# Other gates and another order in the lead-in of a fused attention and ternary-projection kernel on eight cores

## What is computed

```python
xn = _layernorm(x)
q = xn @ w_q + b_q; k = xn @ w_k + b_k; v = xn @ w_v + b_v     # [2, 16384, 1024]
scores = einsum(q, k of positions s-3 .. s+3) / 8              # outside the row: -inf
out = (softmax(scores) applied to v) @ w_o + b_o
scale = maximum(mean(abs(weight)), 1e-5)
w_ternary = clip(round(weight / scale), -1, 1)
result = x + out + xn @ (w_ternary * scale).T
```

## Time and profile before

| | us |
|---|---|
| median of 3 runs (range) | 695.19 (694.86 to 695.31) |
| the profiled execution | 696.35 |
| its span, slowest core (5) | 694.8 |
| spans of the 8 cores | 688.6 to 694.8 |
| PE busy | 644.1 (93%) |
| DVE busy | 434.4 (63%) |
| ACT busy | 375.5 (54%) |

### The profile page before, as it was taken

How to read it: one execution, slowest core, us unless ns; L and a number is a source line. 1 busy time by engine, 2 the same in 40 slices (tenths; PEclk the granted TensorE clock), 3 DMA queues, 4 the chain that set the end, 5 groups by cost and what they waited for, 6 DMA issues and landing times.

```text
span 694.8 us, 11677 instructions; the slowest of 8 cores (688.6 to 694.8 us)
## 1 busy us (share of the span) xinstructions
PE 644.1 (93%) x3890; PEld 299.8 (43%) x3890; DVE 434.4 (63%) x534; ACT 375.5 (54%) x1418; POOL 88.6 (13%) x52
## 2 busy tenths in 40 slices
PE   1669983999999999999999999999899999999996
PEld 1234431444444444444444444444344444455542
DVE  6225398686666667666665666666666755466663
ACT  3333465475555565656555555556556555555572
POOL 1202000221111111111111010011011111111110
PEclk9969996899999999999999999999999999999999
DMA  7699973768554444557563654544353442334423
GB/s 167 158 158 323 166 124 84 213 166 230 137 135 104 120 132 123 110 130 144 131 139 88 152 137 137 137 109 126 86 127 94 109 76 81 92 102 126 123 62 92
DMA packets 129947, 91.19 MB, mean 131 GB/s; under 512 B 107872, under 2 KB 116192, under 8 KB 129888
## 3 DMA queue, kind: packets, MB, share of 16 engines
q1 hardware_dynamic: 121440, 82.05, 45.9%
q0 software_dynamic: 8448, 8.39, 8.8%
HBM read 55.82 MB, written 16.78 MB: 104 GB/s over the span
## 4 chain that ended last, share of the span: by engine, by line
PE 83%; DVE 6%; DMA 4%; ACT 3%; issue 3%; DVEq 0%; SPq 0%; POOL 0%; ACTq 0%; POOLq 0%
PE p_p L284 16%; PE p_f L452 15%; PE p_p L302 15%; PE p_f L468 15%; PE p_p L327 15%; PE p_a L415 3%; PE p_s L355 3%; ACT sm L385 2%; DMA wq_b<-wq 1%; DVE sm L370 1%; DMA x<-x 1%; DMA sm<-x 1%; DVE bst L205 1%; DVE brow L534 1%; DVE wft_b L537 1%
## 5 line engine op out<-in xcount | busy, mean ns | idle before, releaser
L385 ACT ACTIVATE sm<-sm,nmx 122x128 f32<-122x128 f32 x544 | 210.9, 389 | 14.4 <-DVE nmx L377 14.4
L481 POOL TENSOR_TENSOR xr<-xr,brow 128x1024 f32<-128x1024 f32 x32 | 76.0, 2376 | 515.8 <-DMA xr<-x 452.3
L284 PE MATMUL p_p<-xnt,wq_b 128*128 128x488 bf16 (+1 forms) x576 | 129.2, 373 | 3.8 <-DMA wq_b<-wq 2.6
L327 PE MATMUL p_p<-wv_b,xnt 128*128 128x512 bf16 x544 | 124.5, 382 | 0.0
L302 PE MATMUL p_p<-xnt,wk_b 128*128 128x494 bf16 (+1 forms) x576 | 123.2, 361 | 0.0
L292 ACT ACTIVATE qt<-p_p,bq 128x488 bf16<-128x488 f32 (+1 forms) x72 | 46.5, 646 | 139.5 <-PE p_p L284 139.5
L452 PE MATMUL p_f<-wft_b,xnt 128*128 128x512 bf16 x496 | 114.7, 385 | 0.7 <-DVE xr L486 0.7
L468 PE MATMUL p_f<-wo_b,att 128*128 128x512 bf16 x496 | 113.2, 379 | 0.7 <-ACT att L432 0.7
L370 DVE TENSOR_TENSOR sm<-p_s,mk_sb 122x1024 f32<-122x1024 f32 x68 | 82.9, 1220 | 43.5 <-PE p_s L355 43.4
L385 ACT ACTIVATION_READ_ACCUMULATOR sm<-sm,nmx 122x1 f32 x544 | 102.4, 188 | 0.0
L340 ACT CAST v<-p_p 128x512 bf16<-128x512 f32 x68 | 39.0, 575 | 104.7 <-PE p_p L327 104.7
(11 more groups left out here) (62 smaller groups left out, 279.2 us busy)
## 6 DMA issues: line engine op xcount, KB each, us to landing
xr<-x SPq DMA_DIRECT2D x32, 512.0 KB, 4.7
x<-x SPq DMA_DIRECT2D x31, 512.0 KB, 4.5
out<-xr SPq DMA_DIRECT2D x31, 512.0 KB, 3.3
wq_b<-wq POOLq DMA_DIRECT2D x4, 512.0 KB, 9.1
wk_b<-wk POOLq DMA_DIRECT2D x4, 512.0 KB, 16.8
xr<-wft SPq DMA_DIRECT2D x4, 512.0 KB, 9.6
wv_b<-wv POOLq DMA_DIRECT2D x4, 512.0 KB, 16.0
wo_b<-wo POOLq DMA_DIRECT2D x4, 512.0 KB, 24.8
```

The source lines that it names most:

```text
L284: q.do("tensor", lambda e, k=k: e.matmul(bank[:, 0:m], w_b["wq"][:, k * H + 128 * c:k * H + 128 * c + 128], rows_of(b, k, BQ * b + 3, m), ...
L327: q.do("tensor", lambda e, k=k: e.matmul(bank, rows_of(b, k, TQ * i, KW), w_b["wv"][:, k * H + 512 * jh:k * H + 512 * jh + 512], start=(k ...
L385: q.do("scalar", lambda e, h=h: e.activation(sm[hf][0:TQ, KW * h:KW * h + KW], sm[hf][0:TQ, KW * h:KW * h + KW], AF.Exp, bias=nmx[hf][0:TQ ...
L481: q.do("gpsimd", lambda e: e.tensor_tensor(xr[t % NR][:, :], xr[t % NR][:, :], brow[:, :], ALU.add), ("xrb", t))
```

## The change

Each weight piece gets a semaphore of its own, so that an instruction can wait for the first piece of a half. POOL issues all four pieces of `wq` once x tile 0 has landed, and `wk` once tile 5 has. SP's tile 4 waits for piece (1, 0) of `wq`, the third, and the `wft` loads for piece (0, 0) of `wk`, the first. PE does all eight query jobs of block 0 first, then the eight of block 1, then key jobs in the order block 0 columns 0 to 3, block 1 columns 0 to 3, block 0 columns 4 to 7, block 1 columns 4 to 7, with the two halves of `scores(0)` among them. `wf_scale`, the `weights` of window 0 and the terns move with them, and tile 8's statistics stand ahead of the key jobs rather than in step 0. The waits elsewhere are the same with the new names.

```diff
@@ -163,10 +163,13 @@
         def weight_load(n, half, parts=(0, 1)):
             cols = slice(512 * half, 512 * half + 512)
             for k in parts:
-                q.dma("gpsimd", f"{n}{half}", lambda e, k=k: e.dma_start(
+                q.dma("gpsimd", f"{n}{half}{k}", lambda e, k=k: e.dma_start(
                     w_b[n][:, 4 * k * H:(4 * k + 4) * H].rearrange("p (c n) -> p c n", c=4, n=H)[:, :, cols],
                     w_h[n][512 * k:512 * k + 512, cols].rearrange("(c p) n -> p c n", c=4, p=128)),
-                    ("w", n, half))
+                    ("w", n, half, k))
+
+        def weight(n, half):
+            return [("w", n, half, k) for k in range(2)]
 
         def constant_load():
             q.dma("sync", "cb", lambda e: e.dma_start(bias[:, :], bias_h[:, :]), "bias")
@@ -279,7 +282,7 @@
         def q_job(b, c):
             n, bank = next_bank()
             m = TQ * nwin(b)
-            q.need("tensor", ("w", "wq", c // 4), *[("xnt", b, r) for r in tiles_of(b)])
+            q.need("tensor", *weight("wq", c // 4), *[("xnt", b, r) for r in tiles_of(b)])
             for k in range(8):
                 q.do("tensor", lambda e, k=k: e.matmul(
                     bank[:, 0:m],
...
@@ -562,11 +565,10 @@
         for r in (1, 2, 3):
             x_load(r)
         constant_load()
-        q.need("gpsimd", ("x", 1))
-        weight_load("wq", 0, (0,))
-        q.need("gpsimd", ("x", 2))
-        weight_load("wq", 0, (1,))
-        q.need("sync", ("w", "wq", 0))
+        q.need("gpsimd", ("x", 0))
+        weight_load("wq", 0)
+        weight_load("wq", 1)
+        q.need("sync", ("w", "wq", 1, 0))
         x_load(4)
         consts()
         stats(0)
@@ -578,27 +580,13 @@
             xn_by_pe(r - 1, 0)
         bias_forms()
         normalise(3)
+        xn_by_pe(3, 0, 1)
         for r in (5, 6, 7):
             x_load(r)
-        q.need("gpsimd", ("x", 6))
-        weight_load("wq", 1)
+        q.need("gpsimd", ("x", 5))
         weight_load("wk", 0)
         weight_load("wk", 1)
-        xn_by_pe(3, 0, 1)
-        for c in range(4):
-            q_job(0, c)
-            if c >= 1:
-                stats(3 + c)
-                rstd(3 + c)
-                normalise(3 + c)
-            if c >= 2:
-                xn_by_pe(2 + c, 1)
-        stats(7)
-        rstd(7)
-        normalise(7)
-        xn_by_pe(6, 1)
-        xn_by_pe(7, 1)
-        q.need("sync", ("w", "wk", 0))
+        q.need("sync", ("w", "wk", 0, 0))
         for k in range(8):
             wf_load(k)
         q.need("gpsimd", ("wf", 5))
@@ -606,41 +594,58 @@
         weight_load("wv", 1)
         weight_load("wo", 0)
         weight_load("wo", 1)
+
+        for c in range(8):
+            q_job(0, c)
+            if c >= 4:
+                stats(c)
+                rstd(c)
+                if c >= 5:
+                    normalise(c - 1)
+                if c >= 6:
+                    xn_by_pe(c - 2, 1)
+        normalise(7)
         for r in range(8, 8 + NX):
             x_load(r)
+        xn_by_pe(6, 1)
+        xn_by_pe(7, 1)
+        for c in range(8):
+            q_job(1, c)
         for k in range(8):
             wf_abs(k, "vector")
+        stats(8)
+        rstd(8)
+        for c in range(4):
+            k_job(0, c, "scalar")
+        scores(0, 0)
+        mask_max(0, 0)
+        for c in range(4):
+            k_job(1, c, "scalar")
+            if c >= 1:
+                exps(0, 0, ((0, 1), (2, 3, 4), (5, 6, 7))[c - 1])
+        for c in range(4, 8):
+            k_job(0, c, "scalar")
+        scores(0, 1)
+        mask_max(0, 1)
+        k_job(1, 4, "scalar")
+        wf_scale()
         terns = list(enumerate((6, 7, 4, 5, 0, 1, 2, 3)))
 
         def some_terns(lo, hi):
             for j, k in terns[lo:hi]:
                 wf_tern(j, k)
 
-        for b, c in ([(1, c) for c in range(4)] + [(0, c) for c in range(4, 8)]
-                     + [(1, c) for c in range(4, 8)]):
-            q_job(b, c)
-        for c in range(8):
-            k_job(0, c, "scalar")
-        scores(0, 0)
-        mask_max(0, 0)
-        k_job(1, 0, "scalar")
-        k_job(1, 1, "scalar")
-        wf_scale()
-        some_terns(0, 2)
-        scores(0, 1)
-        mask_max(0, 1)
-        some_terns(2, 4)
-        for c in range(2, 8):
+        weights(0, 0)
+        some_terns(0, 4)
+        for c in range(5, 8):
             k_job(1, c, "scalar")
-            exps(0, (c - 2) // 3, ((0, 1), (2, 3, 4), (5, 6, 7))[(c - 2) % 3])
-            if c == 5:
-                weights(0, 0)
-                some_terns(4, 6)
+            exps(0, 1, ((0, 1), (2, 3, 4), (5, 6, 7))[c - 5])
+        weights(0, 1)
+        some_terns(4, 6)
         v_job(0, 0)
         v_evict(0, 0)
         v_job(0, 1)
         v_evict(0, 1)
-        weights(0, 1)
         e_transpose(0, 0)
         e_transpose(0, 1)
 
@@ -654,9 +659,6 @@
         def layer_norm_step(s):
             b, r = 2 + s // BW, stats_of_step(s)
             if r is not None:
-                if s == 0:
-                    stats(r)
-                    rstd(r)
                 normalise(r)
                 if s % BW == 0:
                     xn_by_dma(b, r - 1)
```

More of the change, by code:

```diff
@@ L105, in build_program @@
     tile_of = {out_step(t): t for t in range(NO)}
-    slots = (["cm", "cb", "ci", "bo"] + [f"{n}{k}" for n in ("wq", "wk", "wv", "wo") for k in range(2)] + [f"x{k}" for k in range(5)] + [f"r{k}" for k in range(NR)]
+    slots = (["cm", "cb", "ci", "bo"] + [f"{n}{k}{j}" for n in ("wq", "wk", "wv", "wo") for k in range(2) for j in range(2)] + [f"x{k}" for k in range(5)] + [f"r{k}" for k in range(NR)]
              + [f"o{k}" for k in range(NR)] + [f"t{k}{j}" for k in range(3) for j in range(RT)] + [f"te{k}" for k in range(2)]
@@ L299, in k_job @@
             m = TQ * nwin(b) + KW - TQ
-            q.need("tensor", ("w", "wk", c // 4), *[("xnt", b, r) for r in tiles_of(b)])
+            q.need("tensor", *weight("wk", c // 4), *[("xnt", b, r) for r in tiles_of(b)])
             for k in range(8):
@@ L324, in v_job @@
             n, bank = next_bank()
-            q.need("tensor", ("w", "wv", jh), *[("xnt", b, r) for r in tiles_of(b)])
+            q.need("tensor", *weight("wv", jh), *[("xnt", b, r) for r in tiles_of(b)])
             for k in range(8):
@@ L459, in o_proj @@
             acc = p_out(t)
-            q.need("tensor", ("w", "wo", 0), ("w", "wo", 1), ("att", i, 0))
+            q.need("tensor", *weight("wo", 0), *weight("wo", 1), ("att", i, 0))
             order = [(k, jh) for k in range(8) for jh in range(2)]
@@ L542, in bias_half @@
             n, bank = next_bank()
-            q.need("tensor", ("w", "wo", jh), "bvb")
+            q.need("tensor", *weight("wo", jh), "bvb")
             for k in range(8):
```

## The result

The changed kernel takes 697.37 us (median of 14 executions), the kernel before 695.33 us on the same chip. Two of the 14 took over 712 us with a lower granted clock on cores of one die; without them the median is 696.83, and every ratio and every other time here is taken from executions without such a fall. The ratio is 1.0026, 95% interval 1.0015 to 1.0038: slower by 1.8 us, little but clear of noise. The forecast was 689.2, in a range of 686.0 to 692.2, with 0.06 for slower. The profiled execution took 699.43 us, its slowest core is 0. It is the slowest of the other twelve, so its core 0 shows the loss near its largest.

A forecast was written before the change was run, and what follows sets the result against it. Bounds: the lead-in to PE's unbroken stretch and DVE's queue from the first mask. 5.4 us less, with D's shift, left core 1 slowest at 688.9 against 694.8; 695.19 - 5.9 = 689.3, said as 689.2, range 686 to 692.2.

The forecast's parts named there:

- The new D: D is the start of PE's unbroken stretch: 42.2 on core 5 and 42.0 on core 1, before 43.93 and 41.21.
- The gates' gain: Lead-in: with weights issued earlier, PE's first query job no longer waits for `wq` half 0, before 2.59 us on core 5.
- the first job: PE's first query job waits for x tile 3's copy: 21.1 on core 5, 20.1 on core 1, 1.2 us lost to weights.
- From D to the mask of half 1: PE's 8 query jobs, 12 key jobs and two scores up to DVE's mask of window 0's second half: 36.8 us.
- DVE's queue: From the mask of half 1 to window 2's: 40.2 less 2.5 (mask pair), 2.5 (tile 8) and 0.9 (exponentials), 34.3 us.
- The wait ahead of L519: PE, with one key job covering DVE's way from the mask of half 1 to the sum: about 1.5 us, costed at nothing.
- The sum without the step below: D to window 2's mask 71.1 rather than 76.5, 5.4 us less; with D's shift, 7.1 on core 5, 4.6 on core 1.
- Later weights: Later `wk` and `wft` loads: `wft` issued by 34 to 37, last there by 56 to 60, `rstd(8)` still in time; cost nothing.
- rivals B: Key evictions: tile 8 lands at 63 rather than 61, PE's three banks fill, about 2 us later, 691.3; chance 0.09.
- signs of being wrong: A key eviction waiting for `rstd(8)`, x tile 3 landing past 15 us, or a DVE queue not shorter because of ACT's exponentials.
- Rival C: Tile 8 lands near 69.4 as before, ACT is free 8.6 us after 63, slower than before at 697.9 us; chance 0.05.
- Sharing of the queues: x tiles 1 to 3 beside weights: 1.2 us lost, not the 2.6 of even turns; the `wft` row was read against those.

The follow-up runs named there:

- run 1: The changed kernel with tile 8's statistics and `rstd` back in step 0: 695.06 us, ratio 0.9999 to the kernel before.
- run 5: The changed kernel with tile 8 loaded ahead of the `wft` blocks and its statistics and `rstd` ahead of the eight `wf_abs` sums: 690.45 us, ratio 0.9924.
- run 6: As run 5, with the first scores of window 0 one key job later, behind `k_job(1, 0)`: 690.06 us, ratio 0.9922.
- run 11: Run 5's kernel with all block 0 key jobs first (686.07 us), plus one block 1 key job ahead of the second half's scores: 685.48 us.
- run 8: The kernel before with only tile 8's statistics and `rstd` moved from step 0 to behind the `wf_abs` sums, ahead of the key jobs: 695.38 us, ratio 0.9996.
- run 10: Run 5's kernel with all block 0 key jobs first (686.07 us), plus tile 4's load behind the first `wq` piece, not the third: 688.58 us.
- run 2: The changed kernel with tile 8 loaded ahead of the eight `wft` loads, statistics left where the change has them: 699.05 us, ratio 1.0051.
- run 12: The kernel before with the change's gates alone, except that tile 4 waits for both pieces of `wq` half 0 as before: 698.98 us, ratio 1.0042.

## Why the prediction was wrong, point by point

**The new D: right, in part by luck.** 42.2 and 42.0 forecast on cores 5 and 1; 42.63 and 41.07 measured. The gates' gain was counted from core 5, where D had been 43.93. The mean over the cores was 41.1, and no other core was above 41.54: tile 4 took 6.8 us from its ask to its statistics on core 5 and 3.5 to 5.2 on the others. The 1.7 us that I gave core 5 were no other core's. At the first job errors cancel. The last copy ahead of it is a pair (18.31 on core 0, two copies in 1.93 us), as the row also says, and I had read one of 1.0. The tiles lost 0.6 us or less to the weights on cores 0, 1 and 5, not 1.2. And half 0 of `wq`, put at 16.6, came only at 20.9 on core 5, half a microsecond behind the pair.

**From D to the mask of half 1: 36.8 forecast, 37.9 without the pause (runs 1 and 5).** Missed, by 1.1 us, were the waits of 0.91 and 1.02 us of the scores, which stand directly behind the key job whose eviction they read. Half 0's scores read the keys of the columns 0 to 3. In the old order they stood behind the job of column 7, four jobs after the last key that they read; in the new one directly behind it, and so do half 1's. I counted the products and not this distance; run 6 put one job ahead of half 0's scores and run 11 one ahead of half 1's, and each time that wait was gone. The two waits add up to 1.9; what gives 0.8 of it back wasn't taken apart.

**DVE's queue: right.** 34.3 forecast, 33.41 measured, on every core. The first mask pair out of it was forecast at 2.5; between before and run 1, which also differ in the order of the queue, it is 2.9 (40.2 to 37.3). Tile 8 with ACT's wait was put at 3.4 and is worth 3.9 (37.3 to 33.4, and 40.2 to 36.3 in run 8).

**The wait ahead of L519: right.** 1.5 forecast, 1.10 measured, and no later mask or product shows it.

**The sum without the step below: right.** D to window 2's mask was forecast at 71.1; run 5 has 113.1 - 41.8 = 71.3, and 690.45 us, inside the forecast. That it fits to 0.2 us is luck: the two terms above miss by 1.1 one way and 0.9 the other.

**"Later weights": the step that failed.** It said: "ACT must have done tile 8's `rstd` before it evicts the first key jobs: with three banks it is in time until about 63, and it comes at 60 to 62.5. Cost nothing, cover about 2 us." The mechanism was named, as rivals B and C, and a key eviction that waits for `rstd(8)` was among the signs of being wrong. The term was put at nothing and measured 7.5 us on the way to half 1's mask, because its sizes were wrong, the deadline most of all.

- Late by the gates' chain. `wq`'s third piece, SP's gate for tile 4, was put at 19.9 and came at 22.4 to 23.7; tile 4 was there at 29.09 on core 0, `wk` was asked for at 31.75 and not 28, the `wft` loads at 39.63 and not by 34 to 37. From the ask to the last sum it took 23.8 us (39.63 to 63.38). Before it had been 19.2, and 34 to 37 with 56 to 60 leaves about 22 to 23. This lateness is that of four cores, 0, 2, 5 and 7: `wft` asked for at 39.1 to 40.4, `rstd(8)` at 66.5 to 67.6. On 1, 3, 4 and 6 they are 35.4 to 36.5 and 60.9 to 62.9, nearly as forecast, and PE stood 2.3 to 4.8 us even there.
- Late by DVE's order. I followed tile 8's landing and asked when it would come. The statistics stand behind the last `wf_abs`, and start 1.4 to 2.7 us after that begins: `rstd(8)` at 60.89 on core 4 and at 66.97 on core 0. Tile 8's own landing adds 0.3 to 1.4 us of DVE's wait on six cores and nothing on two.
- The deadline was earlier. PE stops when the third key job is done, 18.4 to 20.8 us after D (at 62.87 on core 0, the latest after D), and ACT's two activations and one eviction must be done by then, 1.4 us from `rstd(8)` to PE's start. So `rstd(8)` had to begin by 61.5 on core 0, and by 58 to 62.3 over all cores, not by 63. On the cores 1, 3, 4 and 6 this makes nearly all of the pause.
- The price of a miss was counted once. The pauses are 2.26 to 5.49 us, mean 4.4; D to the mask of half 1 grew by 7.5. Nearly all of the other 3.1 are products at the lower clock level: behind the pause up to half 1's scores the cores whose clock fell need up to 4.0 us more than core 4, whose clock did not, and the mean over all eight is 2.9. Rival C had 697.9 us for a pause of 8.6 us; the kernel came close to it with pauses of at most 5.5 and the clock.

**Sharing of the queues: the weighing went the wrong way.** I took the row of 51 to 52 us of the earlier trace rows as evidence against an even sharing. It shows a start, not a share: a load that is asked for while the weight queue is full has its first packets 3 to 4 us later. For the `wft` loads of the change on core 0, asked for at 39.63, there is none up to 43.6, and for tile 4 of run 10, asked for at 16.57, none up to 20; before, with no weights in the queues, tile 4's come within 1.0 us on cores 0 and 1 and after 2 on core 5. From then on the turns are even. In the changed kernel, core 0, 50 to 56 us, by queue (packets, MB, share):

```profile
q1 hardware_dynamic: 376, 1.38, 66.1%
q0 software_dynamic: 373, 0.37, 40.6%
```

That is one packet for one packet, while both have work. A `wft` packet is about 3.7 KB and one of the weights 1 KB (1.38 MB by 376, 0.37 by 373), so the loads keep most of the bytes and still lose half of the turns. Run 10 has the same with the x tiles, 229 packets beside 231 in 24 to 28 us. The Trainium skill, DMA: Bandwidth & Descriptors, section "Queues, rings and completion order", says that each DMA engine goes round its queues a packet at a time; this trace agrees, in that the counts come out equal. By it the `wft` blocks, asked for with three pieces of `wk` still ahead, pay one turn for each of their packets as long as these last.

**Accounting.** Mean over cores, mask of window 2 against before: D +0.5, D to half 1's mask 45.4 against 36.0 to the first mask before, +9.4, and the queue 33.4 against 40.2, -6.8. That is +3.1 us (117.3 to 120.4). The time rose by 1.5 to 1.8: the block behind that mask took 572.4 us on average and 574.1 before, and what shortened it stays open.

## What to carry to other kernels

When an instruction moves up in a program, ask what stands directly ahead of it on its own engine, and not only when its input lands: run 2 brought the input early and gained nothing, run 5 moved the instruction ahead of the sums and gained 8.6 us over it. Compute the deadline and the arrival for every core, since the launch ends with the core that misses: half the cores in run 8 gained, and the time did not. And where PE stops, look at the granted clock behind the stop as well: the time at the lower level belongs to its price.

## What the runs showed of the hardware

- The granted clock behind a stop was not the same on all cores: behind a pause of 2.26 us (core 4) the next key job took 1.83 us, behind 5.49 us (core 0) 3.45 us, with a granted clock of 0.50, the lower level, over the next 6.64 us; on core 4 it stayed at 1.00. The Trainium skill, TensorE: Matmul & The Clock Gate, section "HAM oscillation — how this bites in real kernels", describes such a fall behind waits for DMA; here the wait was for ACT, and the row agrees.
- The same load in the same place takes 4.3 us from its ask to its first use with an idle queue beside it (tile 4, before, core 0) and 8.8 us beside the pieces of `wq` (run 12, core 0), of which about 3.0 pass before its first packet.
- Once both queues have work, they send equal numbers of packets (376 beside 373 in 6 us), at about 3.7 KB and 1 KB a packet.
